# Eight PSUM banks shared out anew in a two-layer transformer kernel with three attentions

## The chip, the cores and the metric

The kernel runs on one core of one Trainium2 chip. The metric is the device time of one execution in microseconds; for the kernel before, three executions are known.

## The reference

64 sequences of 128 tokens with 128 features pass through two layers. The first has three parts: self-attention with rotary embedding, cross-attention to 77 context tokens, and an MLP; the second is one more cross-attention. Each part starts with a layer norm, scaled and shifted per sequence. Cut to what matters:

```python
def attn(q, k, v, mask):                      # 16 heads of 8 features
    s = einsum('bqhd,bkhd->bhqk', q, k) / sqrt(8)
    s = where(mask, s, lowest)
    return einsum('bhqk,bkhd->bqhd', softmax(s), v)

x = x + g_msa * (attn(rope(xn @ Wq), rope(xn @ Wk), xn @ Wv, mask) @ Wo)   # 128 keys
x = x + g_x   * (attn(xc @ cq, ctx @ ck, ctx @ cv, kv_mask) @ co)          # 77 keys
x = x + g_mlp * (gelu(xm @ W1 + b1) @ W2 + b2)
x = x + attn(xq @ Wq1 + bq, cn @ Wk1 + bk, cn @ Wv1 + bv) @ Wp + bp        # 77 keys
```

## The kernel before

The activations stay in SBUF, features on partitions (`c.xt`). `two_layers` calls phases one after the other; each is a block with one program per engine, written out by hand in order and joined by semaphores. There are setup, load, norms, three attentions (named `sa`, `ca` and `xa`; the text calls them the first, second and third), the MLP and the store.

An attention works in **groups** of 4 sequences (16 groups), **steps** of one sequence (4 per group) and **units** of half a step, 8 of the 16 heads (8 per group, 128 in all). The loops on all engines run over the same number `u`, here called slot; slot `8i + n` is the n-th slot of group i. In slot u the engines do this:

- TensorE: for even u `turn_max` (line 446) transposes the row maxima of a step; `natural(u + 3)` (line 419) makes scores with the queries on partitions, for the maxima alone; `transposed(u)` (line 452) makes the scores again with the keys on partitions and adds the negated maxima; `values(u - 1)` (line 477) multiplies the exponentials of the unit before with the values; and `project` (line 394) does one projection, where the table `slot_jobs` (line 375) has one.
- ScalarE: for even u `keep_max` (line 605), `exponentials(u)` (line 618), for even u `invert` (line 611, two instructions for 1/sum), in slot 8i `take_values` (line 593, four copies of the projected values into `vz`), and parts of splitting q and k into bf16 pieces.
- VectorE: `maxima(u + 3)` (line 530), `read_out` of a step in odd slots (line 539, `den` and `vv` out of the values' bank), and `take` or `add_out` (lines 509, 547), which read a projection of slot u - 1.
- GpSimd splits the maxima and q and k into pieces and multiplies `vv` with 1/sum (`normalise`, line 661). SyncE moves the pieces of q and k into `stacks`, group by group.

The projections of a group stand in these slots: in the first attention `q`, `qr`, `k`, `kr` (`r` for the rotated ones) in slots 0 to 3 for the group two further on, in the other two `q` in slot 1 and `k` in slot 3; in all of them `o`, the output projection of the group before, in slot 5, and `v`, the values of the next group, in slot 7.

The 8 PSUM banks: a pair `ps_nat` for the first scores, a pair `ps_st` for the transposed ones, two banks `ps_pj` that projections take in turn, and two `ps_po` that steps take in turn for the values' output, with the transposed maxima in the same bank. Who waits for whom on TensorE follows from that:

```python
if number[job] >= 2:                      # project: the reader of the job two before
    before, ib = jobs[number[job] - 2]
...
if u > 0:                                 # transposed: the exponentials of the unit before
    pe.wait_ge(exped, u)
...
if step >= 2:                             # values: step - 2 read out
    pe.wait_ge(po_read, step - 1)
```

Of the kernel before, what the change touches and what calls it, by code (L numbers as in the profile page):

```python
# [29 lines left out]
H, HD = 16, 8  # L30
# [316 lines left out]
def attention_phase(nc, c, name, ctx, *, nk, kv_src, wq, wk, wv, wo, rotate=False, q_bias=None,  # L347
# [38 lines left out]
    takes = {job: n for n, job in enumerate(j for j in jobs if j[0] in kinds)}  # L386
    pj = lambda job: c.ps_pj[number[job] % 2]

    with nc.Block() as block:
        @block.tensor  # L390
        def _(pe):
            t = nc.tensor

            def project(job):
                kind, i = job
                if number[job] >= 2:
                    before, ib = jobs[number[job] - 2]
# [48 lines left out]
            def turn_max(step):  # L446
                pe.wait_ge(max_split, 4 * step + 4)
                if step >= 2:
                    pe.wait_ge(po_read, step - 1)
                t.transpose(c.turned_max[step % 2], c.nm[:, step % 2, :], c.eye_bf[:]).then_inc(max_turned, 1)  # L450

            def transposed(u):
                step, p = u // 2, u % 2
                i, j = step // G, step % G
                par = i % NB
                if u > 0:
                    pe.wait_ge(exped, u)
                if pair_mask:
                    for h in range(2):
                        t.matmul(c.ps_st[h][0:nk, :], c.eye_bf[:], c.mask_t[:].unsqueeze(1).broadcast_to([128, 4, S]),  # L460
                                 start=True, stop=False, skip_group_check=True)
                for g in range(4):
                    for h in range(2):
                        at = pair(2 * p, g)
                        t.matmul(c.ps_st[h][0:nk, S * g:S * g + S], kst[half(h), par, at, nk * j:nk * j + nk],  # L465
                                 qst[half(h), par, at, S * j:S * j + S],
                                 start=g == 0 and not pair_mask, stop=False, skip_group_check=True)
                if p == 0:
                    pe.wait_ge(max_kept, step + 1)
                for g in range(4):  # L470
                    for h in range(2):
                        m = t.matmul(c.ps_st[h][0:nk, S * g:S * g + S], c.pick_bf[half(h), 4 * (2 * p + h) + g:4 * (2 * p + h) + g + 1].broadcast_to([64, nk]),  # L472
                                     c.mt[half(h), step % 2, :], start=False, stop=g == 3, skip_group_check=True)
                        if g == 3:
                            m.then_inc(st_full, 1)

            def values(u):
# [28 lines left out]
        def _(dve):  # L506
            v = nc.vector

            def take(job):
                kind, i = job  # L510
                x = 0 if kind[0] == "q" else 1
                bank = pj(job)
                dve.wait_ge(pj_full, number[job] + 1)
# [25 lines left out]
            def read_out(step):  # L539
                bank = c.ps_po[step % 2]  # L540
                dve.wait_ge(pv_done, 2 * step + 2)
# [5 lines left out]
            def add_out(i):  # L547
                job = ("o", i)
                dve.wait_ge(pj_full, number[job] + 1)
                if gate is None:  # L550
                    xs = c.xt[:, NT * i:NT * i + NT]
                    v.scalar_tensor_tensor(out=xs, in0=pj(job)[:], scalar=out_bias, in1=xs, op0=ALU.add, op1=ALU.add).then_inc(added, 1)
                else:
                    for b in range(G):
                        n = G * i + b
                        xs = c.xt[:, S * n:S * n + S]
                        v.scalar_tensor_tensor(out=xs, in0=pj(job)[:, S * b:S * b + S], scalar=c.mod[:, gate, n:n + 1],
                                               in1=xs, op0=ALU.mult, op1=ALU.add).then_inc(added, 1)
# [18 lines left out]
        def _(act):  # L577
# [15 lines left out]
            def take_values(i):  # L593
                job = ("v", i)
                act.wait_ge(pj_full, number[job] + 1)
                if i >= 2:
                    act.wait_ge(pv_done, PER * (i - 1))
                src = pj(job)[0:nk, :].rearrange("p (b t f) -> p b t f", b=G, t=H // 2)
                for hh in range(4):
# [5 lines left out]
            def keep_max(step):  # L605
                act.wait_ge(max_turned, step + 1)
                if step >= 2:
                    act.wait_ge(st_full, 4 * (step - 1))
                a.activation(c.mt[:, step % 2, :], c.turned_max[step % 2], ACT.Copy).then_inc(max_kept, 1)  # L609

# [7 lines left out]
            def exponentials(u):  # L618
# [4 lines left out]
                bias = c.key_bias[0:nk, step:step + 1] if key_mask else 0.0  # L623
                a.activation(c.p[0:nk, 2 * p:2 * p + 2, :].rearrange("p h n -> p (h n)"), c.st_pair[0:nk, :], ACT.Exp, bias=bias).then_inc(exped, 1)  # L624

# [199 lines left out]
def two_layers(nc, ins, out):  # L825
    with ExitStack() as ctx:
# [68 lines left out]
        c.ps_nat = [c.nat_pair[:, 0:512], c.nat_pair[:, 512:1024]]  # L895
        c.ps_st = [c.st_pair[:, 0:512], c.st_pair[:, 512:1024]]
        c.ps_pj = [ps("ps_pj0"), ps("ps_pj1")]

        c.ps_po = [ps("ps_po0"), ps("ps_po1")]
        c.turned_max = [bank[:, 2 * S:2 * S + S // 2].bitcast(BF16) for bank in c.ps_po]  # L900
        c.turned_mask = c.ps_po[0][:].bitcast(BF16)

# [60 lines left out]
```

## Time and profile before

| | us |
|---|---|
| median of 3 runs | 1566.06 |
| lowest and highest run | 1566.05, 1567.51 |
| the profiled execution | 1563.82 |
| its span | 1562.2 |
| TensorE busy (matmuls) | 1337.8 |
| ScalarE busy | 905.3 |
| VectorE busy | 805.7 |
| GpSimd busy | 688.2 |

The profiled execution is one execution of its own; its time is 2.2 us below the median and 1.6 above its span. Busy time counts overlapping instructions once. PE is TensorE, PEld its weight loads, ACT ScalarE, DVE VectorE, POOL GpSimd. "Idle before" is the time in which an engine did nothing ahead of an instruction, with what ended it. An instruction's recorded end can overlap the next one's start by a few hundredths of a us.

### The profile page before, as it was taken

Reading aid. Unit: us, or ns where it says so; the run is one execution under the profiler, and the core shown is the slowest. Engines: PE = TensorE matmul, PEld = TensorE weight load, DVE = VectorE, ACT = ScalarE, POOL = GpSimd, SP = SyncE. Lnnn points to the kernel's source line nnn. Section 1 sums busy time; section 2 is a strip of 40 time slices with the busy share of each in tenths; the row PEclk is TensorE's granted clock in tenths of the full one; section 3 lists DMA queues with packets and bytes.
Section 4 is the critical chain, followed back from the end, with each engine's and each line's share of the span. In section 5 each row is a group of like instructions: output and inputs, shape, how many; then the busy total and the mean of one; then the engine's idle time right before and its main releaser. Section 6 shows DMA issues by size and latency. Waiting matters only on the chain. (4 is left out here: it accounts for less than half of the span.)

```text
span 1562.2 us, 44242 instructions
## 1 busy us (share of the span) xinstructions
PE 1337.8 (86%) x17952; PEld 746.4 (48%) x17952; DVE 805.7 (52%) x1772; ACT 905.3 (58%) x1692; POOL 688.2 (44%) x1405
## 2 busy tenths in 40 slices
PE   2584999999999988499999998889987488888885
PEld 2531555555555442255555555334433355555563
DVE  4263565656665546255555554522167355565553
ACT  0171555555555547277777777644476477777773
POOL 0004556565656520466666663001100566666640
PEclk9996999999999999699999999899998799999996
DMA  2502534344343500444444442000000555555423
GB/s 82 151 1 54 101 64 92 73 84 82 73 92 63 102 2 1 87 89 84 83 84 83 81 83 37 0 0 0 0 1 1 99 93 100 95 96 92 89 46 108
DMA packets 136124, 103.44 MB, mean 66 GB/s; under 512 B 13913, under 2 KB 135666, under 8 KB 135922
## 3 DMA queue, kind: packets, MB, share of 16 engines
q1 hardware_dynamic: 135922, 100.62, 32.8%
q8 instruction: 142, 2.33, 0.6%
q14 instruction: 60, 0.49, 0.1%
HBM read 9.08 MB, written 4.19 MB: 8 GB/s over the span
## 5 line engine op out<-in xcount | busy, mean ns | idle before, releaser
L535 DVE TENSOR_REDUCE negmax<-ps_nat 128x8 f32<-128x616 f32 (+1 forms) x384 | 361.1, 940 | 403.8 <-PE ps_nat L442 159.9
L624 ACT ACTIVATE p<-ps_st 128x1024 f32<-128x1024 f32 (+1 forms) x256 | 260.5, 1018 | 181.5 <-PE ps_st L472 179.5
L489 PE MATMUL ps_po<-p,vz 77*32 77x128 f32 (+1 forms) x6144 | 248.5, 279 | 26.6 <-issue 24.6
L431 PE MATMUL ps_nat<-stacks 64*128 64x77 bf16 (+1 forms) x3072 | 134.2, 209 | 58.0 <-DMA stacks<-parts 51.7
L667 POOL TENSOR_TENSOR ot<-vv,den 128x256 f32<-128x256 f32 x192 | 139.5, 727 | 100.4 <-ACT den L616 99.3
L465 PE MATMUL ps_st<-stacks 64*77 64x128 bf16 (+1 forms) x3072 | 158.0, 223 | 24.7 <-ACT p L624 22.4
L489 PEld LDWEIGHTS ps_po<-p,vz 77*32 77x32 f32 (+1 forms) x6144 | 145.9, 109 | 64.2 <-issue 29.9
L624 ACT ACTIVATE p<-ps_st,key_bias 77x1024 f32<-77x1024 f32 x128 | 141.5, 1105 | 59.9 <-PE ps_st L472 59.7
L653 POOL CAST nm<-negmax 128x32 bf16<-128x32 f32 x192 | 40.0, 209 | 289.9 <-DVE negmax L535 289.8
L431 PEld LDWEIGHTS ps_nat<-stacks 64*128 64x128 bf16 x3072 | 78.1, 97 | 179.3 <-issue 147.0
L679 POOL TENSOR_TENSOR whole<-whole,parts 128x512 f32<-128x512 f32 x96 | 98.3, 1024 | 137.4 <-ACT parts L587 137.4
L465 PEld LDWEIGHTS ps_st<-stacks 64*77 64x77 bf16 (+1 forms) x3072 | 97.1, 107 | 127.5 <-issue 68.7
L472 PE MATMUL ps_st<-mt,pick_bf 64*77 64x128 bf16 (+1 forms) x3072 | 151.7, 219 | 0.0
L609 ACT ACTIVATE mt<-ps_po 128x128 bf16<-128x128 bf16 x192 | 52.8, 275 | 128.3 <-PE ps_po L450 128.2
L472 PEld LDWEIGHTS ps_st<-mt,pick_bf 64*77 64x77 bf16 (+1 forms) x3072 | 106.9, 108 | 2.5 <-ACT mt L609 0.3
L408 PE MATMUL ps_pj<-ot,wo 128*128 128x512 f32 x192 | 100.4, 648 | 7.1 <-POOL ot L667 7.1
L687 POOL TENSOR_TENSOR parts<-whole,parts 128x512 bf16<-128x512 f32 x96 | 98.5, 1026 | 0.0
L674 POOL TENSOR_TENSOR whole<-part 128x512 f32<-128x512 f32 x32 | 40.6, 1269 | 121.7 <-DVE part L519 121.7
L680 POOL COPY parts<-parts 128x1024 bf16<-128x1024 bf16 x96 | 88.4, 921 | 0.0
L544 DVE STREAM_SHUFFLE den<-ps_po 128x256 f32<-128x256 f32 x192 | 85.7, 446 | 0.0
L616 ACT ACTIVATE den<-den 128x256 f32<-128x256 f32 x192 | 80.0, 417 | 6.1
L587 ACT ACTIVATE parts<-whole 128x512 bf16<-128x512 f32 x96 | 53.6, 559 | 50.0 <-DMA stacks<-parts 29.5
(142 smaller groups left out, 2144.0 us busy)
## 6 DMA issues: line engine op xcount, KB each, us to landing
stacks<-parts SPq DMA_DIRECT2D x512, 128.0 KB, 3.2
stacks<-parts SPq DMA_DIRECT2D x256, 77.0 KB, 2.6
p<-in_x_dram SPq DMA_DIRECT2D x16, 256.0 KB
out_dram<-p SPq DMA_DIRECT2D x16, 256.0 KB, 2.4
p<-in_ctx_dram SPq DMA_DIRECT2D x16, 154.0 KB
ht<-in_L_xcond_adaLN_W_dram SPq DMA_DIRECT2D x1, 576.0 KB
w<-in_L_xcond_mlp_W_dram SPq DMA_DIRECT2D x2, 256.0 KB
wqkv<-in_L_xcond_qkv_W_dram SPq DMA_DIRECT2D x1, 192.0 KB
```

Of the source, the lines that this page charges most:

```text
L408: m = t.matmul(bank[:], wo[:, p, :], c.ot[:, i % 2, p, :], start=p == 0, stop=p == 1)
L431: m = t.matmul(c.ps_nat[h][:, nk * g:nk * g + nk], qst[half(h), par, at, S * j:S * j + S], kst[half(h), par, at, nk * j:nk * j + nk], star ...
L465: t.matmul(c.ps_st[h][0:nk, S * g:S * g + S], kst[half(h), par, at, nk * j:nk * j + nk], qst[half(h), par, at, S * j:S * j + S], start=g = ...
L472: m = t.matmul(c.ps_st[h][0:nk, S * g:S * g + S], c.pick_bf[half(h), 4 * (2 * p + h) + g:4 * (2 * p + h) + g + 1].broadcast_to([64, nk]), ...
L489: m = t.matmul(bank[32 * g:32 * g + 32, S * p:S * p + S], c.vz[0:nk, i % 2, j, g, 32 * hh:32 * hh + 32], c.p[0:nk, hh, S * g:S * g + S], s ...
L535: v.tensor_reduce(c.negmax[:, step % 2, 8 * p:8 * p + 8].rearrange("p (h g) -> p h g", h=2), c.nat_pair[:].rearrange("p (h n) -> p h n", h ...
L544: v.stream_shuffle(c.den[:, step % 2, :], bank[:, 0:2 * S], DEN_ROWS).then_inc(den_here, 1)
L624: a.activation(c.p[0:nk, 2 * p:2 * p + 2, :].rearrange("p h n -> p (h n)"), c.st_pair[0:nk, :], ACT.Exp, bias=bias).then_inc(exped, 1)
L667: p.tensor_tensor(c.ot[:, i % 2, :, S * j:S * j + S], c.vv[:, step % 2, :].rearrange("q (p n) -> q p n", p=2), c.den[:, step % 2, :].rearr ...
L679: p.tensor_tensor(c.whole[:, x, w], c.whole[:, x, w], c.parts[:, x, hi[0], w], ALU.subtract).then_inc(rest, 1)
L680: p.tensor_copy(c.parts[:, x, hi[1]:hi[2] + 1:hi[2] - hi[1], w], c.parts[:, x, hi[0]:hi[0] + 1, w].broadcast_to([128, 2, width[x]]))
L687: p.tensor_tensor(c.parts[:, x, LOW[x], w], c.whole[:, x, w], c.parts[:, x, md[0], w], ALU.subtract).then_inc(split[x], 1)
```

## The change

The transposed scores get two pairs of banks that units take in turn (`c.st[u % 2]`), the values' output one bank (`c.po`, the transposed maxima with it) and the projections one bank (`c.pj`). The waits follow: `transposed(u)` waits for the exponentials of unit u - 2 instead of u - 1; `values` for the read-out of step - 1 instead of step - 2; `project` for the reader of the last job instead of the last but one. VectorE's `read_out` moves to the front of its slot, ahead of `take` (first attention) and `maxima`. The phases outside the attentions use the same banks under other names. The core of the diff:

```diff
-    pj = lambda job: c.ps_pj[number[job] % 2]
...
             def project(job):
                 kind, i = job
-                if number[job] >= 2:
-                    before, ib = jobs[number[job] - 2]
+                if number[job] >= 1:
+                    before, ib = jobs[number[job] - 1]
                     if before == "v":
                         pe.wait_ge(values_kept, ib + 1)
                     elif before == "o":
                         pe.wait_ge(added, N_ADD * (ib + 1))
                     else:
                         pe.wait_ge(taken, takes[before, ib] + 1)
-                bank = pj(job)
+                bank = c.pj
...
-                t.transpose(c.turned_max[step % 2], c.nm[:, step % 2, :], c.eye_bf[:]).then_inc(max_turned, 1)
+                t.transpose(c.turned_max, c.nm[:, step % 2, :], c.eye_bf[:]).then_inc(max_turned, 1)
...
             def transposed(u):
-                if u > 0:
-                    pe.wait_ge(exped, u)
+                if u > 1:
+                    pe.wait_ge(exped, u - 1)
...
-                        t.matmul(c.ps_st[h][0:nk, S * g:S * g + S], kst[half(h), par, at, nk * j:nk * j + nk],
+                        t.matmul(c.st[u % 2][h][0:nk, S * g:S * g + S], kst[half(h), par, at, nk * j:nk * j + nk],
...
             def values(u):
-                    if step >= 2:
-                        pe.wait_ge(po_read, step - 1)
-                bank = c.ps_po[step % 2]
+                    if step >= 1:
+                        pe.wait_ge(po_read, step)
+                bank = c.po
...
             for u in range(FIRST, LAST):
+                if in_range(u - 2) and u % 2 == 1 and u >= 3:
+                    read_out((u - 3) // 2)
                 if rotate and u - 1 in slot_jobs:
                     read(slot_jobs[u - 1])
                 if in_range(u + AHEAD):
                     maxima(u + AHEAD)
-                if in_range(u - 2) and u % 2 == 1 and u >= 3:
-                    read_out((u - 3) // 2)
                 if not rotate and u - 1 in slot_jobs:
                     read(slot_jobs[u - 1])
...
-        c.nat_pair = ctx.enter_context(nc.psum_tensor("ps_nat", [128, 1024], F32))
-        c.st_pair = ctx.enter_context(nc.psum_tensor("ps_st", [128, 1024], F32))
-        c.ps_pj = [ps("ps_pj0"), ps("ps_pj1")]
-        c.ps_po = [ps("ps_po0"), ps("ps_po1")]
+        pairs = [ctx.enter_context(nc.psum_tensor("ps_" + n, [128, 1024], F32)) for n in ("nat", "st0", "st1", "rest")]
+        halves = lambda pair: [pair[:, 0:512], pair[:, 512:1024]]
+        c.ps_nat, c.ps_st, c.ps_pj = halves(pairs[0]), halves(pairs[1]), halves(pairs[2])
+        c.st = [halves(pairs[1]), halves(pairs[2])]
+        c.po, c.pj = halves(pairs[3])
```

How this moves instructions and waits is best seen in two places. The first is TensorE's queue in the first attention, slot 8 (scores, values of unit 7, projection of `q`, then the next `natural`), with the semaphores that each waits for. Before:

```order
L460 MATMUL ps_st<-mask_t,eye_bf 128x512 [waits sa_exped]
...
L472 MATMUL ps_st<-mt,pick_bf 128x128 [waits sa_max_kept]
...
L489 MATMUL ps_po1<-p,vz 32x128 [waits sa_exped]
...
L416 MATMUL ps_pj0<-ht,wqkv 128x512 [waits sa_taken]
L431 MATMUL ps_nat<-stacks 128x128 [waits sa_maxed]
...
L489 MATMUL ps_po0<-p,vz 32x128 [waits sa_po_read,sa_values_kept,sa_exped]
...
L416 MATMUL ps_pj1<-ht,wrot 128x512 [waits sa_values_kept]
```

And changed (every line number is one lower, `ps_rest` holds `po` and `pj`):

```order
L459 MATMUL ps_st0<-mask_t,eye_bf 128x512 [waits sa_exped]
...
L471 MATMUL ps_st0<-mt,pick_bf 128x128 [waits sa_max_kept]
...
L488 MATMUL ps_rest<-p,vz 32x128 [waits sa_exped]
...
L415 MATMUL ps_rest<-ht,wqkv 128x512 [waits sa_values_kept]
L430 MATMUL ps_nat<-stacks 128x128 [waits sa_maxed]
...
L488 MATMUL ps_rest<-p,vz 32x128 [waits sa_po_read,sa_values_kept,sa_exped]
...
L415 MATMUL ps_rest<-ht,wrot 128x512 [waits sa_taken]
```

No matmul has moved; the wait for `values_kept` (ScalarE's `vz`) has moved from `qr` to `q`, ahead of the next `natural`.

The second place is VectorE's queue in the third attention, slots 8i+1 to 8i+3. Before:

```order
L535 TENSOR_REDUCE negmax<-ps_nat 128x8 [waits xa_max_split,xa_nat_full]
L544 STREAM_SHUFFLE den<-ps_po1 128x256 [waits xa_out_ready,xa_pv_done]
L545 COPY vv<-ps_po1 128x256
L535 TENSOR_REDUCE negmax<-ps_nat 128x8 [waits xa_nat_full]
L526 TENSOR_SCALAR whole<-ps_pj0,vec 128x512 [waits xa_split_q,xa_pj_full]
L535 TENSOR_REDUCE negmax<-ps_nat 128x8 [waits xa_max_split,xa_nat_full]
L544 STREAM_SHUFFLE den<-ps_po0 128x256 [waits xa_out_ready,xa_pv_done]
L545 COPY vv<-ps_po0 128x256
```

And changed:

```order
L543 STREAM_SHUFFLE den<-ps_rest 128x256 [waits xa_out_ready,xa_pv_done]
L544 COPY vv<-ps_rest 128x256
L534 TENSOR_REDUCE negmax<-ps_nat 128x8 [waits xa_max_split,xa_nat_full]
L534 TENSOR_REDUCE negmax<-ps_nat 128x8 [waits xa_nat_full]
L525 TENSOR_SCALAR whole<-ps_rest,vec 128x512 [waits xa_split_q,xa_pj_full]
L543 STREAM_SHUFFLE den<-ps_rest 128x256 [waits xa_out_ready,xa_pv_done]
L544 COPY vv<-ps_rest 128x256
L534 TENSOR_REDUCE negmax<-ps_nat 128x8 [waits xa_max_split,xa_nat_full]
```

The read-out (shuffle and copy) has passed the reduction of its slot; the reading of a projection, here `q`, stands ahead of it as before.

## Rows read from the trace of the kernel before

**Rows 1.** The page's busy times: engine, busy us (share of the span), instructions.
```profile
PE 1337.8 (86%) x17952; PEld 746.4 (48%) x17952; DVE 805.7 (52%) x1772; ACT 905.3 (58%) x1692; POOL 688.2 (44%) x1405
```

**Rows 2.** Waits in total (us, times, longest), then the group of line 450 (busy | idle).
```profile
PEld ps_st L465 <- ACT p L624: 57.6, 139, 1.0
...
L450 PE MATMUL ps_po<-eye_bf,nm 128*128 128x128 bf16 x192 | 42.5, 221 | 3.8 <-DVE vv L545 3.7
```

**Rows 3.** TensorE's timeline, first attention: projections of `q`. Columns: start, us.
```profile
158.81 1.13 PE L416 MATMUL ps_pj<-ht,wqkv 128*128 128x512 f32 x2
...
265.04 1.13 PE L416 MATMUL ps_pj<-ht,wqkv 128*128 128x512 f32 x2
...
506.81 1.12 PE L416 MATMUL ps_pj<-ht,wqkv 128*128 128x512 f32 x2
```

**Rows 4.** ScalarE's timeline, first attention, in the same slots.
```profile
159.87 0.78 ACT L601 ACTIVATE vz<-ps_pj 128x128 f32<-128x128 f32 x4
...
264.60 1.02 ACT L624 ACTIVATE p<-ps_st 128x1024 f32<-128x1024 f32 x1 [1.60 <-PE ps_st L472]
...
266.28 0.76 ACT L601 ACTIVATE vz<-ps_pj 128x128 f32<-128x128 f32 x4
...
508.05 0.76 ACT L601 ACTIVATE vz<-ps_pj 128x128 f32<-128x128 f32 x4
```

**Rows 5.** Timeline, first attention: a read-out that TensorE waits for.
```profile
175.32 0.41 DVE L545 COPY vv<-ps_po 128x256 f32<-128x256 f32 x1
...
175.88 0.22 PE L450 MATMUL ps_po<-eye_bf,nm 128*128 128x128 bf16 x1 [0.53 <-DVE vv L545]
```

**Rows 6.** TensorE's timeline, third attention, slots 8i+2, 8i+3, 8i+5, 8i+7.
```profile
1421.66 0.32 PE L431 MATMUL ps_nat<-stacks 64*128 64x77 bf16 x8
...
1422.44 0.65 PE L489 MATMUL ps_po<-p,vz 77*32 77x128 f32 x16
1423.02 0.32 PE L431 MATMUL ps_nat<-stacks 64*128 64x77 bf16 x8
1423.65 0.42 PE L465 MATMUL ps_st<-stacks 64*77 64x128 bf16 x8 [0.32 <-ACT p L624]
...
1424.22 0.64 PE L489 MATMUL ps_po<-p,vz 77*32 77x128 f32 x16
...
1428.19 0.64 PE L489 MATMUL ps_po<-p,vz 77*32 77x128 f32 x16
...
1433.29 0.65 PE L489 MATMUL ps_po<-p,vz 77*32 77x128 f32 x16
```

**Rows 7.** VectorE's timeline, third attention, the same stretch.
```profile
1422.77 0.74 DVE L526 TENSOR_SCALAR whole<-ps_pj,vec 128x512 f32<-128x512 f32 x1
...
1424.14 0.45 DVE L544 STREAM_SHUFFLE den<-ps_po 128x256 f32<-128x256 f32 x1
1424.49 0.40 DVE L545 COPY vv<-ps_po 128x256 f32<-128x256 f32 x1
...
1426.68 0.53 DVE L528 TENSOR_SCALAR whole<-ps_pj,vec 128x308 f32<-128x308 f32 x1
...
1431.83 0.74 DVE L552 SCALAR_TENSOR_TENSOR xt<-ps_pj,bp,xt 128x512 f32<-128x512 f32 x1
```

**Rows 8.** Timeline, second attention: VectorE's `add_out` and TensorE's values, slot 8i+7.
```profile
751.94 1.12 DVE L557 SCALAR_TENSOR_TENSOR xt<-ps_pj,mod,xt 128x128 f32<-128x128 f32 x4
...
753.56 0.64 PE L489 MATMUL ps_po<-p,vz 77*32 77x128 f32 x16
```

**Rows 9.** TensorE's gap in the timeline, then windows: us, busy times, PEclk (1.00 is 2.4 GHz).
```profile
547.35 0.61 PE L431 MATMUL ps_nat<-stacks 64*128 64x128 bf16 x8 [2.42 <-DMA stacks<-parts]
...
547.20:550.60 3.40, 3.25 (x28) 1.58 (x28) 1.64 (x4) 0.00 (x0) 0.00 (x0) 0.50 0.02 5
584.75:588.10 3.35, 3.35 (x4) 0.90 (x4) 0.00 (x0) 0.00 (x0) 0.00 (x0) 0.50 0.00 0
1475.65:1479.00 3.35, 3.35 (x35) 1.59 (x27) 0.43 (x1) 0.67 (x2) 0.00 (x0) 0.50 0.72 132
```

More of the change, by code:

```diff
@@ L455, in transposed @@
                 par = i % NB
[L456 to L457 removed]
+                if u > 1:
+                    pe.wait_ge(exped, u - 1)
                 if pair_mask:
                     for h in range(2):
[L460 removed]
+                        t.matmul(c.st[u % 2][h][0:nk, :], c.eye_bf[:], c.mask_t[:].unsqueeze(1).broadcast_to([128, 4, S]),
                                  start=True, stop=False, skip_group_check=True)
@@ L471, in transposed @@
                     for h in range(2):
-                        m = t.matmul(c.ps_st[h][0:nk, S * g:S * g + S], c.pick_bf[half(h), 4 * (2 * p + h) + g:4 * (2 * p + h) + g + 1].broadcast_to([64, nk]),
+                        m = t.matmul(c.st[u % 2][h][0:nk, S * g:S * g + S], c.pick_bf[half(h), 4 * (2 * p + h) + g:4 * (2 * p + h) + g + 1].broadcast_to([64, nk]),
                                      c.mt[half(h), step % 2, :], start=False, stop=g == 3, skip_group_check=True)
@@ L511, in take @@
                 x = 0 if kind[0] == "q" else 1
-                bank = pj(job)
+                bank = c.pj
                 dve.wait_ge(pj_full, number[job] + 1)
@@ L539, in read_out @@
             def read_out(step):
-                bank = c.ps_po[step % 2]
+                bank = c.po
                 dve.wait_ge(pv_done, 2 * step + 2)
@@ L551, in add_out @@
                     xs = c.xt[:, NT * i:NT * i + NT]
-                    v.scalar_tensor_tensor(out=xs, in0=pj(job)[:], scalar=out_bias, in1=xs, op0=ALU.add, op1=ALU.add).then_inc(added, 1)
+                    v.scalar_tensor_tensor(out=xs, in0=c.pj[:], scalar=out_bias, in1=xs, op0=ALU.add, op1=ALU.add).then_inc(added, 1)
                 else:
@@ L556, in add_out @@
                         xs = c.xt[:, S * n:S * n + S]
-                        v.scalar_tensor_tensor(out=xs, in0=pj(job)[:, S * b:S * b + S], scalar=c.mod[:, gate, n:n + 1],
+                        v.scalar_tensor_tensor(out=xs, in0=c.pj[:, S * b:S * b + S], scalar=c.mod[:, gate, n:n + 1],
                                                in1=xs, op0=ALU.mult, op1=ALU.add).then_inc(added, 1)
@@ L608, in keep_max @@
                     act.wait_ge(st_full, 4 * (step - 1))
-                a.activation(c.mt[:, step % 2, :], c.turned_max[step % 2], ACT.Copy).then_inc(max_kept, 1)
+                a.activation(c.mt[:, step % 2, :], c.turned_max, ACT.Copy).then_inc(max_kept, 1)
             def invert(step):
@@ L623, in exponentials @@
                 bias = c.key_bias[0:nk, step:step + 1] if key_mask else 0.0
-                a.activation(c.p[0:nk, 2 * p:2 * p + 2, :].rearrange("p h n -> p (h n)"), c.st_pair[0:nk, :], ACT.Exp, bias=bias).then_inc(exped, 1)
+                a.activation(c.p[0:nk, 2 * p:2 * p + 2, :].rearrange("p h n -> p (h n)"), c.st_pairs[u % 2][0:nk, :], ACT.Exp, bias=bias).then_inc(exped, 1)
             steps = (((4, 0, split_high), (6, 0, split_mid), (6, 1, split_high), (8, 1, split_mid)) if rotate
@@ L892, in two_layers @@
         c.vec_row = VEC_ROW
-        c.nat_pair = ctx.enter_context(nc.psum_tensor("ps_nat", [128, 1024], F32))
-        c.st_pair = ctx.enter_context(nc.psum_tensor("ps_st", [128, 1024], F32))
-        c.ps_nat = [c.nat_pair[:, 0:512], c.nat_pair[:, 512:1024]]
-        c.ps_st = [c.st_pair[:, 0:512], c.st_pair[:, 512:1024]]
-        c.ps_pj = [ps("ps_pj0"), ps("ps_pj1")]
-        c.ps_po = [ps("ps_po0"), ps("ps_po1")]
-        c.turned_max = [bank[:, 2 * S:2 * S + S // 2].bitcast(BF16) for bank in c.ps_po]
-        c.turned_mask = c.ps_po[0][:].bitcast(BF16)
+        pairs = [ctx.enter_context(nc.psum_tensor("ps_" + n, [128, 1024], F32)) for n in ("nat", "st0", "st1", "rest")]
+        halves = lambda pair: [pair[:, 0:512], pair[:, 512:1024]]
+        c.vec_row = VEC_ROW
+        c.nat_pair, c.st_pairs = pairs[0], pairs[1:3]
+        c.ps_nat, c.ps_st, c.ps_pj = halves(pairs[0]), halves(pairs[1]), halves(pairs[2])
+        c.st = [halves(pairs[1]), halves(pairs[2])]
+        c.po, c.pj = halves(pairs[3])
+        c.turned_max = c.po[:, 2 * S:2 * S + S // 2].bitcast(BF16)
+        c.turned_mask = c.po.bitcast(BF16)
         setup_phase(nc, c, ins, ctx)
```

2 lines of the change are left out of this document (1 added, 1 removed).

## The prediction

> **What bounds the kernel now.** I read the page's busy shares first: TensorE is busy for 86% of the span [rows 1], more than any other engine, so only time that TensorE spends waiting can be won, and every wait added to its queue is paid. Then I read the waits and the grouped instructions, since the change is meant to loosen one wait of TensorE, the one for the exponentials (`exped`). The wait that can be seen is small: 57.6 us of idle weight loads in 139 waits, and where the matmuls themselves idle the timeline of the third attention puts it at 0.32 us each [rows 2, 6]. The first attention has none of it in its steady groups: its timeline of TensorE is closed, and the project of `q` in slot 8i follows the values without a gap [rows 3]. So the gain can only lie in the second and third attention, and anything that holds TensorE in the first one goes to the end of the kernel in full.
>
> **The bank of the projections, first attention.** Before, a projection waits for the reader of the projection two before it. Now it waits for the last one. The projections stand in slots 0, 1, 2, 3 (`q`, `qr`, `k`, `kr`), 5 (`o`) and 7 (`v`) of each group, and only one neighbour matters: `v` of slot 8i-1 is read by ScalarE in slot 8i (`take_values`, line 601), and there it stands behind the exponential of the same slot and the two instructions of `invert`. `q` of slot 8i must now wait for it, where only `qr`, a slot later, did. In the group shown ScalarE starts its exponential at 264.60 and the four copies to `vz` at 266.28, which end 0.76 later at 267.04 [rows 4]. `q` started at 265.04 [rows 3]. The handover from a reader to the next matmul took 0.15 us where VectorE's copy ended at 175.73 and TensorE started at 175.88 [rows 5]. The new stall is 267.04 + 0.15 - 265.04 = 2.15 us. It comes for `v` 0 to 13, 14 times; the first one is 159.87 + 0.78 + 0.15 - 158.81 = 1.99, the last (508.05 against 506.81) is 2.15 again [rows 3, 4]. Together 1.99 + 13 x 2.15 = **29.9 us**. ScalarE can't come earlier, since its chain starts when TensorE has filled the scores of slot 8i, which stands ahead of `q`. Queued behind `q` are the maxima's scores for VectorE and the scores of slot 8i+1, so nobody works in the gap. Bounds: 14 x 2.00 = 28 without any handover, 14 x 2.35 = 33 with 0.2 more for a weight load that can't be hidden.
>
> The other pairs have room. `qr` waits for `take` of `q`, which VectorE does (0.7 us) while TensorE does a whole slot of some 3.5 us; `v` waits for `add_out` of slot 6. In the second and third attention `q` stands in slot 8i+1, behind the values of step 4i, which wait for the same `vz` already: nothing is added there.
>
> **What the gap does to TensorE's clock.** The granted clock is at 2.4 GHz through nearly all of the first attention. After its one long gap, 2.42 us for the stacks, it fell to 1.2 GHz for 3.4 us, and in the third attention it fell once after a gap of 0.81 us [rows 9], while about 30 gaps of that size stand in the second and third attention. The other gap of its kind, at the end of this attention, was followed by 1.2 GHz too, the window from 584.75 on [rows 9]. My gaps of 2.15 us are nearer to the 2.42 that brought the clock down than to the 0.81 that mostly didn't. I take 9 falls in 14. A fall costs at most half of 3.4 us, 1.7; I take 1.6, because work bound by weight loads slows less. Together 9 x 1.6 = **14.4 us**; bounds 0 and 14 x 1.7 = 24. The Trainium skill (TensorE: Matmul & The Clock Gate, section HAM oscillation) holds only idle stretches longer than any of these for dangerous; by it this term is nothing, and the sum would be 14.4 lower. The trace does not agree with it for the gap of 2.42.
>
> **The second pair of banks for the scores, third attention.** In a slot with an even number TensorE goes from the first scores to the values in 1422.44 - 1421.66 = 0.78 us; in an odd one, where it waits for the exponential, it takes 1424.22 - 1423.02 = 1.20 [rows 6]. So 0.42 us could be won in odd slots. But the values of the odd slot now have another wait, `po_read`: there is one bank for their output, and VectorE must have read out the step before. VectorE's two read-out instructions take 1424.49 + 0.40 - 1424.14 = 0.75 us, and in its queue they stand behind what it does in the slot before. The next instruction on VectorE starts some 0.07 us ahead of the recorded end of the one before. Slot 3: behind `take` of `q`, which ends at 1422.77 + 0.74 - 0.07 = 1423.44; read out by 1424.19, values at 1424.34 instead of 1424.22: 0.12 lost. Slot 5: behind `take` of `k`, 1426.68 + 0.53 - 0.07 = 1427.14, so 1428.04 instead of 1428.19: 0.15 won. Slot 7: behind `add_out`, 1431.83 + 0.74 - 0.07 = 1432.50, so 1433.40 instead of 1433.29: 0.11 lost [rows 6, 7]. Slot 1: the values wait for `vz`, on the same ScalarE chain as before: nothing. That is 0.08 lost per group, 15 groups, **1.2 us**. Bound on the good side: 3 x 0.42 x 15 = 19 us won, if VectorE were in time everywhere. That the read-out stands ahead of the maxima costs VectorE's reduction up to 0.75 us, but TensorE needs it only after the projection of that odd slot, so it stays hidden.
>
> The Trainium skill (Perfetto Trace Analysis, section Matmuls) wants independent groups of matmuls rotated through different banks, so that reading one overlaps filling the next. The change follows this for the scores and gives it up for the values and the projections; by this case's rows the second weighs more.
>
> **Second attention.** The same walk for slot 7: `add_out` is four instructions of 1.12 us together, ends at 751.94 + 1.12 - 0.07 = 752.99, and the values come at 752.99 + 0.75 + 0.15 = 753.89 instead of 753.56 [rows 8]: 0.33 lost. Slots 3 and 5 have room and win their wait for the exponential, which is too short to show as idle of the matmuls; I take 0.1 each. 0.13 x 15 = **2.0 us** lost.
>
> **Ends of the phases.** The transposed maxima waited 3.8 us in all for VectorE's `vv`, in groups that lack a projection [rows 2]; with the read-out first in its slot these waits go, but about a third of them stand ahead of a wait for the stacks that takes them back: 2.5 won. The first steps of the third attention win about 1 more. At the start of the first attention `qr` must wait for `take` of `q`, one reading of 0.7 us and a handover: 1 us lost. Net **2.5 us won**. Norms, MLP and store only change names of banks: nothing.
>
> **The sum.** 29.9 + 14.4 + 1.2 + 2.0 - 2.5 = 45.0 us. On the profiled execution's 1563.82 that is 1608.8. The median of the runs is 2.2 above that execution, so the forecast is 1566.06 + 45.0 = **1611 us**, 2.9% slower.
>
> **The rivals.**
> First, the clock holds in the gaps (3 falls or fewer). For it: some 30 gaps of 0.81 us with one or two falls. Against: the one gap of over 2 us inside this attention. Time: 1611 - 14 = 1597. Its condition is also the skill's rule named above. Chance 0.23.
> Second, the clock falls after every gap: 1611 + 8 to 10 = 1620. For it: both long gaps of this attention were followed by 1.2 GHz. Chance 0.14.
> Third, on the other side: the scores run ahead and every wait for the exponential is won back, at all four odd slots of a group in both later attentions, 15 x 4 x (0.42 + 0.1) = 31, and with the 3.7 at the ends 35, while the clock holds: 1566 + 30 - 35 = 1561, a little faster. For it: these waits are in the trace and the second pair takes them away. Against: VectorE's queue in slots 3 and 7 [rows 7, 8] and `vz` in slot 1. It decides only from a winning of over 0.5 us per odd slot, which is more than these rows hold. Chance 0.05.
> That the second pair does nothing because the values of slot u-1, right behind the scores of slot u, wait for the same exponential is contained in the forecast: it holds for the first attention, where no such wait was.
>
> **How the numbers follow.** The forecast's own case, 4 to 12 falls, has 0.5 and spans 1602 to 1617. The rest, 0.08, is for terms off in size, a third of it within no change. The range takes the first rival with some slack for the bound of 19 us in the third attention, and most of the second: 1590 to 1622. A change under 0.2%, 3 us, can't be told from none in a measurement of this kernel. Faster by more: 0.05 (the third rival). Within: 0.03. Slower by more: 0.92.
>
> **What would show it.** Right: in the first attention TensorE idles some 2 us ahead of `q` of slot 8i, 14 times, released by ScalarE's `vz`; a group there is 29.0 us long instead of 26.9 ((506.81 - 265.04) / 9 from [rows 3]), or some 30.6 where the clock falls behind the gap; rows of 1.2 GHz right behind several of these gaps; in the third attention no idle ahead of the scores for the exponential, but 0.3 to 0.5 ahead of the values, released by VectorE's copy of `vv`; and a group there as long as before within 0.2 us. Wrong: if `q` does not idle, if groups of the third attention are shorter by over 0.5 us, or if the clock stays at 2.4 GHz through the whole first attention.

## The result, and the profile after

| | before | changed |
|---|---|---|
| median, us | 1566.78 | 1610.13 |
| lowest to highest, runs | 1566.05 to 1568.03, 4 | 1606.38 to 1617.32, 4 |
| the profiled execution | 1563.82 | 1609.02 |

The changed kernel is slower: the ratio is 1.0285 with a 95% interval of 1.026 to 1.0309. The forecast was 1611, and 1608.8 for the profiled execution.

To see where the time went I cut both timelines of TensorE into the three attentions, each from its first projection to the start of its last output projection:

| us | before | changed | difference |
|---|---|---|---|
| first attention | 463.88 | 509.52 | +45.6 |
| second attention | 352.10 | 352.09 | 0.0 |
| third attention | 323.35 | 323.13 | -0.2 |

All of the loss lies in the first attention. The waits of the changed kernel, in total (us, times, longest), name most of it:

```profile
PEld ps_rest L415 <- ACT vz L600: 31.4, 14, 2.3
...
PEld ps_rest L488 <- ACT p L623: 30.7, 50, 1.1
...
PE ps_rest L415 <- ACT vz L600: 27.7, 14, 2.0
...
PE ps_rest L488 <- DVE vv L544: 25.9, 61, 0.5
...
PE ps_rest L488 <- ACT vz L600: 21.5, 17, 1.3
```

Line 415 is the projection, line 488 the values. The third row is the new stall, 14 times and 2.0 us at most. The fourth is the other new wait, for VectorE's read-out. The wait of the scores' weight loads for the exponentials, 57.6 us before [rows 2], has all but gone (3.9 us are left); 30.7 us of a wait for the same instruction now stand ahead of the values. The transposed maxima, line 450 before with 3.8 us of idle time [rows 2], have none left:

```profile
L449 PE MATMUL ps_rest<-eye_bf,nm 128*128 128x128 bf16 x192 | 42.7, 222 | 0.0
```

TensorE's timeline of the first attention (start, duration, in brackets the idle time before), the first four projections of `q` in the slots of [rows 3]:

```profile
164.47 1.12 PE L415 MATMUL ps_rest<-ht,wqkv 128*128 128x512 f32 x2 [1.82 <-ACT vz L600]
...
193.08 1.12 PE L415 MATMUL ps_rest<-ht,wqkv 128*128 128x512 f32 x2 [1.99 <-ACT vz L600]
...
222.00 1.12 PE L415 MATMUL ps_rest<-ht,wqkv 128*128 128x512 f32 x2 [1.99 <-ACT vz L600]
...
252.49 1.12 PE L415 MATMUL ps_rest<-ht,wqkv 128*128 128x512 f32 x2 [1.99 <-ACT vz L600]
```

and ScalarE's copies to `vz` ahead of two of them:

```profile
192.27 0.76 ACT L600 ACTIVATE vz<-ps_rest 128x128 f32<-128x128 f32 x4
...
221.19 0.76 ACT L600 ACTIVATE vz<-ps_rest 128x128 f32<-128x128 f32 x4
```

The copies end at 193.03 and 221.95, and `q` starts 0.05 us later. From 193.08 to 222.00 a group takes 28.92 us, from 222.00 to 252.49 it takes 30.49. Before, a group took 26.86. The difference between the two lengths of now is 1.57, and the view of windows says what it is. Its columns: stretch, length; busy time (instructions) of PE, PEld, DVE, ACT, POOL; granted clock; DMA share; GB/s.

```profile
194.10:197.50 3.40, 3.40 (x47) 1.76 (x47) 1.92 (x2) 1.02 (x1) 1.23 (x2) 1.00 0.78 149
223.60:226.90 3.30, 3.30 (x36) 1.67 (x34) 1.48 (x2) 0.70 (x1) 0.66 (x1) 0.50 0.76 143
252.70:256.10 3.40, 3.40 (x47) 1.57 (x47) 1.92 (x2) 0.82 (x2) 1.73 (x2) 1.00 0.78 165
```

Behind the gaps that end at 193.08 and 252.49 the clock stays at 2.4 GHz, behind the one that ends at 222.00 it is at 1.2, and a stretch of about the same length holds 36 matmuls in place of 47. Such a stretch of some 3.4 us follows 11 of the 14 gaps.

The third attention, where [rows 6, 7] were read, on TensorE:

```profile
1418.68 1.98 PE L407 MATMUL ps_rest<-ot,wo 128*128 128x512 f32 x4
...
1428.41 0.64 PE L488 MATMUL ps_rest<-p,vz 77*32 77x128 f32 x16 [1.32 <-ACT vz L600]
...
1432.76 0.65 PE L488 MATMUL ps_rest<-p,vz 77*32 77x128 f32 x16 [0.54 <-DVE vv L544]
...
1436.56 0.65 PE L488 MATMUL ps_rest<-p,vz 77*32 77x128 f32 x16 [0.33 <-DVE vv L544]
1437.14 1.98 PE L407 MATMUL ps_rest<-ot,wo 128*128 128x512 f32 x4
...
1441.77 0.64 PE L488 MATMUL ps_rest<-p,vz 77*32 77x128 f32 x16 [0.54 <-DVE vv L544]
```

and VectorE ahead of the values at 1432.76:

```profile
1431.20 0.74 DVE L525 TENSOR_SCALAR whole<-ps_rest,vec 128x512 f32<-128x512 f32 x1
...
1431.87 0.44 DVE L543 STREAM_SHUFFLE den<-ps_rest 128x256 f32<-128x256 f32 x1
1432.21 0.41 DVE L544 COPY vv<-ps_rest 128x256 f32<-128x256 f32 x1
```

These are `take` of `q`, shuffle and copy. The copy ends at 1432.62, and the values start 0.14 us later. The idle 1.32 us at 1428.41 is the wait for `vz` in slot 8i+1; before, TensorE idled there for 0.81 us. The scores no longer wait, the values do. A group takes 1437.14 - 1418.68 = 18.46 us against 18.41 before (output projections at 1391.93 and 1410.34 there).

### The profile page after: what moved, and what is told of

It is laid out like the page before. It is cut to its first block and busy times, and to the rows that moved or that the text cites. A ratio compares the mean times of both kernels' runs of the same rounds, so it can differ in the third digit from the quotient of the medians.

```text
span 1607.4 us, 44245 instructions
## 1 busy us (share of the span) xinstructions
PE 1354.0 (84%) x17952; PEld 750.4 (47%) x17952; DVE 807.1 (50%) x1772; ACT 904.6 (56%) x1692; POOL 687.8 (43%) x1405
## 5 line engine op out<-in xcount | busy, mean ns | idle before, releaser
L488 PE MATMUL ps_rest<-p,vz 77*32 77x128 f32 (+1 forms) x6144 | 249.2, 280 | 63.5 <-DVE vv L544 25.9
L488 PEld LDWEIGHTS ps_rest<-p,vz 77*32 77x32 f32 (+1 forms) x6144 | 148.2, 109 | 104.1 <-issue 47.1
L608 ACT ACTIVATE mt<-ps_rest 128x128 bf16<-128x128 bf16 x192 | 52.9, 276 | 131.5 <-PE ps_rest L449 131.4
L407 PE MATMUL ps_rest<-ot,wo 128*128 128x512 f32 x192 | 98.7, 638 | 7.1 <-POOL ot L666 7.1
L298 PE MATMUL ps_st<-xt,centre 128*128 128x512 f32 x128 | 72.1, 658 | 16.9 <-DVE p L338 10.0
L543 DVE STREAM_SHUFFLE den<-ps_rest 128x256 f32<-128x256 f32 x192 | 84.8, 441 | 0.0
L438 PE MATMUL ps_nat<-mask_nat,eye_bf 128*128 128x512 bf16 x256 | 84.0, 412 | 0.0
```

Of the source, the lines that this page charges most:

```text
L488: m = t.matmul(bank[32 * g:32 * g + 32, S * p:S * p + S], c.vz[0:nk, i % 2, j, g, 32 * hh:32 * hh + 32], c.p[0:nk, hh, S * g:S * g + S], s ...
L543: v.stream_shuffle(c.den[:, step % 2, :], bank[:, 0:2 * S], DEN_ROWS).then_inc(den_here, 1)
```

## The experiments

Every kernel was timed beside the kernel before on the same chip. Three series were run; the median of before was 1567.41 in the first, 1564.31 in the second and 1565.29 in the third, so where kernels of different series are compared, the difference of the ratios stands beside that of the medians. A kernel "as the changed one, but" has its line numbers from there.

### One projection bank alone

The kernel before with one edit: both names of projection banks lead to one bank, and the wait follows.

```diff
-    pj = lambda job: c.ps_pj[number[job] % 2]
+    pj = lambda job: c.ps_pj[0]
...
-                if number[job] >= 2:
-                    before, ib = jobs[number[job] - 2]
+                if number[job] >= 1:
+                    before, ib = jobs[number[job] - 1]
```

> Only the projections' bank changes: one bank in place of two, each projection waits for the reader of the last one; scores, values' output and VectorE's order stay as before. My theory (the loss is q waiting for vz in the first attention, and the clock falling behind that gap): nearly the whole loss is here. First attention about 45 us longer, 14 gaps of 2.0 us ahead of q, some 11 of them followed by 1.2 GHz; second and third as before; 1605 to 1618 us in all. Rival (the loss comes from the values' single bank or from the new order on VectorE): within 3 us of before, 1567.

Measured: 1616.53 (1614.27 to 1618.55), ratio 1.0336 [1.0305, 1.0366]: 49 us above before by the medians, 53 by the ratio. The waits:

```profile
PEld ps_st L465 <- ACT p L624: 57.9, 139, 1.0
...
PE ps_pj L416 <- ACT vz L601: 27.7, 14, 2.0
```

The first row is nearly as before (57.6), the second is the changed kernel's stall to the tenth of a microsecond; 12 gaps are followed by 1.2 GHz. The first attention takes 513.54 us, 49.7 more than before. The third was 4.3 us longer in this execution as well: nearly all of its groups are as long as before, 18.42 us, but more stretches of 1.2 GHz stand among them. So one bank for the projections explains the loss by itself. What the rest of the change does looks like a small net gain, but the intervals of the two ratios just overlap.

### One values bank alone

The kernel before with one bank for the values' output and the read-out first in its slot; the two projection banks and the one pair for the scores stay.

```diff
-                    if step >= 2:
-                        pe.wait_ge(po_read, step - 1)
+                    if step >= 1:
+                        pe.wait_ge(po_read, step)
...
+                if in_range(u - 2) and u % 2 == 1 and u >= 3:
+                    read_out((u - 3) // 2)
                 if rotate and u - 1 in slot_jobs:
...
-                if in_range(u - 2) and u % 2 == 1 and u >= 3:
-                    read_out((u - 3) // 2)
...
-        c.ps_po = [ps("ps_po0"), ps("ps_po1")]
+        c.ps_po = [ps("ps_po0")] * 2
```

> Only the values' output changes: one bank in place of two, with VectorE's read-out first in its slot; the projections keep two banks, the scores one pair. My theory: nothing in the first attention; in the second 0.33 us more in slot 7 (5 us), in the third 0.1 more in slots 3 and 7 (3.5 us), 2.5 us won where the transposed maxima waited for vv: 1570 to 1575. Rival (the read-out always has room): 1564. Rival (the single bank costs in the first attention too): 1580 or more.

Measured: 1570.92 (1569.24 to 1576.31, 10 runs), ratio 1.0035 [1.0017, 1.0053]. The first attention is 2.1 us shorter than before, the second 3.9 longer, the third 4.5 longer. A group of the second attention takes 20.69 us in place of 20.36, 0.33 more. The timeline of the second attention shows the wait in slot 7, where `add_out` stands ahead of the read-out, beside the wait for the exponentials, which is still there (second fence, the waits):

```profile
753.80 0.65 PE L489 MATMUL ps_po<-p,vz 77*32 77x128 f32 x16 [0.25 <-DVE vv L545]
```

```profile
PE ps_st L465 <- ACT p L624: 24.1, 68, 0.9
```

By the ratios one bank costs 5 us for the values and 53 us for the projections (3.5 and 49 by the medians).

### The second pair of score banks taken back

The changed kernel with one pair for the transposed scores, and its wait.

```diff
-                if u > 1:
-                    pe.wait_ge(exped, u - 1)
+                if u > 0:
+                    pe.wait_ge(exped, u)
...
-        c.nat_pair, c.st_pairs = pairs[0], pairs[1:3]
+        c.nat_pair, c.st_pairs = pairs[0], [pairs[1], pairs[1]]
...
-        c.st = [halves(pairs[1]), halves(pairs[2])]
+        c.st = [halves(pairs[1]), halves(pairs[1])]
```

> The changed kernel with its second pair of banks for the transposed scores taken back (they wait for the exponentials of the unit before again). My theory: the second pair is worth little, since the values wait for VectorE's read-out or for vz nearly as long: 0.1 to 0.15 us in slots 3 and 5 of the later attentions, 3 to 6 us in all, so 1612 to 1617 with the spread that the clock gives. Rival (the second pair wins its 0.42 us per odd slot and hides a larger loss of the single banks): 20 us or more above the changed kernel, 1630 or more.

Measured: 1622.18 (1621.6 to 1623.88), ratio 1.0374 [1.0346, 1.0402]: 12 us above the changed kernel by the medians, 14 by the ratios. The first attention is as long as in the changed kernel (509.84 against 509.52), the second 3.6 us longer, the third 8.8. The waits for ScalarE are back, and those for VectorE have nearly gone behind them:

```profile
PE ps_rest L488 <- DVE vv L544: 3.5, 14, 0.3
...
PE ps_st L464 <- ACT p L623: 22.3, 62, 0.9
```

So the second pair does what it says, and is worth 12 us or more here, two to four times what I had expected. Much of the 8.8 is the clock. At the start of the third attention it stays at 1.2 GHz longer, so that the first `k` inside the slots comes 36.43 us behind the first projection instead of 33.90. Behind that, up to the gap ahead of the last output projection, it falls to 1.2 GHz 6 times where in the changed kernel it falls 3 times, and a group of this attention with such a stretch takes 1.2 us more (19.68 against 18.46). That makes 2.5 + 3 x 1.2 = 6.1; the waits by themselves would then be worth 3.6 + 2.7 = 6.3. This is read from one execution of each kernel and not tested by itself.

### The gap filled

Does the gap cost only its own length, or the clock too? The changed kernel with nine more matmuls of 512 columns ahead of the projection of `q`, which write to a bank that the next scores overwrite. They are extra work that the reference doesn't have; none of the kernel's own is left out.

```diff
                     values(u - 1)
+                if rotate and u % PER == 0 and 0 <= u <= PER * (NG - 3):
+                    for _ in range(9):
+                        t.matmul(c.st[(u + 1) % 2][0], c.eye_bf[:], c.mask_t[:].unsqueeze(1).broadcast_to([128, 4, S]),
+                                 start=True, stop=True, skip_group_check=True)
```

> The changed kernel with nine more matmuls of 512 columns ahead of q in the 14 slots in which it waits for vz; they write into the pair of banks for the next transposed scores, which start anew there, so the result stays. They take some 1.9 us, as long as the gap. My theory: the wait stays as long, but the clock no longer falls, so the first attention is 16 to 18 us shorter than in the changed kernel and the time is 1590 to 1597 (0 to 2 rows of 1.2 GHz in the steady groups). Rival (the time above the gaps comes from something else that follows the stall): 1605 to 1615, as the changed kernel.

Measured: 1595.69 (1594.22 to 1599.93), ratio 1.0209 [1.0172, 1.0245]: 14.4 us below the changed kernel by the medians, 12 by the ratios. The timeline:

```profile
216.21 2.12 PE L503 MATMUL ps_st<-mask_t,eye_bf 128*128 128x512 bf16 x9
218.26 1.13 PE L415 MATMUL ps_rest<-ht,wqkv 128*128 128x512 f32 x2
...
245.13 2.12 PE L503 MATMUL ps_st<-mask_t,eye_bf 128*128 128x512 bf16 x9
247.19 1.12 PE L415 MATMUL ps_rest<-ht,wqkv 128*128 128x512 f32 x2
```

The useless matmuls fill the gap, `q` comes when it did, and the group is 247.19 - 218.26 = 28.93 long, as long as with an empty gap (28.92). But no steady group has 1.2 GHz in it any more, and the first attention is 18.4 us shorter. The clock's term is thereby measured apart from the stall. The time as a whole gains less than 18.4, since the third attention was 3.7 us longer in this execution, most of it by more time at 1.2 GHz.

### The reader brought forward

If what costs is `vz` behind an exponential, then `take_values` in front of it should cure the first attention, with one bank for the projections. I made the edit in both kernels:

```diff
                         keep_max(u // 2)
+                    if at == 0 and i - 2 in range(NG):
+                        take_values(i - 2)
                     exponentials(u)
...
                     invert((u - 4) // 2)
-                if at == 0 and i - 2 in range(NG):
-                    take_values(i - 2)
```

The changed kernel with it:

> The changed kernel with ScalarE's four copies to vz moved ahead of the exponential of their slot (behind the copy of the transposed maxima). My theory: vz is there about 0.7 us after v, before q wants its bank; the first attention loses its 14 gaps and its falls of the clock (45 us), and in the later attentions the values of slot 8i+1 no longer wait for vz (0.8 us and part of the wait for the exponential, 31 groups: 25 to 35 us). 1532 to 1543 us. Rival (q has another reason to wait, or the exponential comes later by the 0.7 us of the copies and TensorE waits for it in turn): 1565 or more.

The kernel before with it:

> The kernel before with the same move of the copies to vz, nothing else. My theory: nothing in the first attention, 0.8 us in each group of the later ones, 25 us: 1541 to 1545 us. If the second pair of banks is of use once vz is early, the changed kernel with the move is faster than this one by 3 to 8 us; if the single banks for values and projections cost more than it wins, it is slower by up to 5. Rival (the copies delay the exponential and nothing is won): 1565.

Measured: the changed kernel 1537.32 (1536.56 to 1544.83), ratio 0.9827 [0.9791, 0.9862]; the kernel before 1539.24 (1538.36 to 1541.22), ratio 0.9827 [0.9794, 0.9859]. Both are faster than either kernel without the edit, the second one by slightly more than I had expected. ScalarE of the changed one, then its TensorE:

```profile
263.35 0.28 ACT L608 ACTIVATE mt<-ps_rest 128x128 bf16<-128x128 bf16 x1 [0.39 <-PE ps_rest L449]
263.52 0.78 ACT L600 ACTIVATE vz<-ps_rest 128x128 f32<-128x128 f32 x4
265.23 1.02 ACT L623 ACTIVATE p<-ps_st 128x1024 f32<-128x1024 f32 x1 [0.93 <-PE ps_st L471]
```

```profile
265.67 1.12 PE L415 MATMUL ps_rest<-ht,wqkv 128*128 128x512 f32 x2
...
292.53 1.13 PE L415 MATMUL ps_rest<-ht,wqkv 128*128 128x512 f32 x2
```

The copies to `vz` end at 264.30, 1.37 us ahead of `q`, in time in which ScalarE waits for scores anyway (0.93 us are left). The gap is gone and the group is 26.86 long again. The gain of the changed kernel over before lies in the later attentions: the second takes 337.09 and the third 313.31 us, 15.0 and 10.0 less. There the values of slot 8i+1 had waited 1.32 us for `vz` (the row at 1428.41 above), and all 3 falls of the clock among the groups of the third attention had come behind that wait; now the wait is gone, no fall is left between 1248 and 1472 us, and the longest wait is another:

```profile
1350.74 0.32 PE L430 MATMUL ps_nat<-stacks 64*128 64x77 bf16 x8 [0.97 <-DMA stacks<-parts]
...
1352.02 1.98 PE L407 MATMUL ps_rest<-ot,wo 128*128 128x512 f32 x4
...
1356.65 0.65 PE L488 MATMUL ps_rest<-p,vz 77*32 77x128 f32 x16 [0.54 <-DVE vv L544]
...
1368.41 0.32 PE L430 MATMUL ps_nat<-stacks 64*128 64x77 bf16 x8 [0.57 <-DMA stacks<-parts]
...
1369.68 1.98 PE L407 MATMUL ps_rest<-ot,wo 128*128 128x512 f32 x4
```

This group takes 17.66 us; the others between 1263 and 1458 us take 17.4 to 18.2. In the kernel before the edit wins 12.0 us in the second attention, 8.5 in the third, and 2.7 in the first, where I had expected nothing.

Is the new sharing of banks of any use once the reader is early? Both kernels again, in the third series.

The changed one:

> The changed kernel with the copies to vz early once more, beside the kernel before with the same move, in five rounds. If the second pair of banks is of use, this one is 2 to 4 us faster; rival: no difference beyond 1 us.

The one of before:

> The kernel before with the copies to vz early once more: 1538 to 1541 us; see the run beside it.

Measured: 1539.49 (1535.3 to 1543.97), ratio 0.983 [0.9805, 0.9855], and 1541.63 (1537.3 to 1543.14), ratio 0.9839 [0.9814, 0.9863]. The difference between the two kernels is 2 us in the same direction both times, but the intervals overlap, so it isn't shown. By the profiles the new sharing wins 3.0 to 3.6 us in the second attention and 1.5 in the third, and loses 1.6 to 2.0 in the first, whose start runs slower (below).

### Two attempts to win the read-out's wait

What is left of the change's cost in the later attentions is the wait for the read-out behind `take` of `q` and `k`. With `q` and `k` in slots 0 and 2, their readers stand elsewhere in VectorE's queue. The early-reader version of the changed kernel, with:

```diff
-    at_slot = dict(zip(kinds, range(4) if rotate else (1, 3)))
+    at_slot = dict(zip(kinds, range(4) if rotate else (0, 2)))
```

> The changed kernel with vz early, and in the second and third attention q and k projected in slots 0 and 2 in place of 1 and 3, so that VectorE reads them in odd slots behind the read-out, not in even slots ahead of it. My theory: the waits of the values for vv in slots 3 and 5 of the third attention go (0.54 and 0.33 us of idle each), but the wait for the stacks in slot 5 (1.1 us now) takes it back, since the splitting of q and k stays where it was: within 3 us of the same kernel without this step, 1534 to 1541. Rival (the read-out's wait is what bounds the third attention): 1520 to 1527.

Measured: 1542.46 (1542.02 to 1543.84), ratio 0.9854 [0.9833, 0.9875]: no gain over 1539.49. The waits for the read-out fell from 28.0 us in 68 to 17.1 in 43, but other waits took their place. The longest is an idle time of 1.24 to 1.35 us ahead of the first scores, for which the trace names no releaser, and three times in the third attention the clock fell behind it. So the read-out's wait alone was not what bound that attention.

Then the splits of ScalarE and GpSimd one slot earlier as well, so that the stacks come sooner:

```diff
-                     else ((2, 0, split_high), (4, 0, split_mid), (4, 1, split_high), (6, 1, split_mid)))
+                     else ((1, 0, split_high), (3, 0, split_mid), (3, 1, split_high), (5, 1, split_mid)))
...
-                     else ((3, 0, take_high), (5, 0, take_mid), (5, 1, take_high), (7, 1, take_mid)))
+                     else ((2, 0, take_high), (4, 0, take_mid), (4, 1, take_high), (6, 1, take_mid)))
```

> As the run before it, with ScalarE's and GpSimd's splitting of q and k one slot earlier as well in the second and third attention, so that the stacks come earlier. My theory (once vz is early, the stacks and the read-out bound the third attention together): both waits go, some 1 us per group and the odd slots of ScalarE are less empty: 1518 to 1530. Rival (ScalarE's splits in odd slots push its exponential, or the stacks are not bound by the splits): 1534 or more.

Measured: 1563.78 (1561.11 to 1571.73, 10 runs), ratio 0.9991 [0.9975, 1.0008]. A clear miss of the 1518 to 1530 that I had expected, and 21 us slower than the version without it. The rows of ScalarE, then of TensorE:

```profile
1422.15 0.63 ACT L586 ACTIVATE parts<-whole 128x512 bf16<-128x512 f32 x1
1422.68 0.26 ACT L608 ACTIVATE mt<-ps_rest 128x128 bf16<-128x128 bf16 x1
```

```profile
1423.00 0.42 PE L471 MATMUL ps_st<-mt,pick_bf 64*77 64x128 bf16 x8 [0.75 <-ACT mt L608]
```

A split of an odd slot now stands ahead of `keep_max` (line 608) of the next even slot, and TensorE waits for the maxima, 58 times and 36.0 us in all; that wait had been 5.2 us in the version without it and 1.5 in the changed kernel. It is the case's own mistake over again, on the same engine: work put in front of a reader that TensorE needs.

## Why the prediction was right

**The stall of `q`**: right in place, releaser and number. Forecast 2.15 us each; the longer groups give 28.92 - 26.86 = 2.06, which is 0.07 more than the idle time shown. With 1.82 + 0.07 = 1.89 for the first that is 13 x 2.06 + 1.89 = 28.7 us against 29.9. What was too large is the handover: 0.15 us by the row of VectorE's copy, 0.05 behind ScalarE's. That ScalarE can't come earlier was wrong as it was put. Its exponential can't, but the copies to `vz` need not stand behind it: put in front they ended 1.37 us ahead of `q`.

**The clock**: right in kind, undersized. 11 gaps brought the clock down where I had taken 9, at 1.57 us each where I had taken 1.6: 17.3 against 14.4. The filled gap gives 18.4 for the same thing. The first rival, that the clock holds, is refuted in this attention: a gap of 2.0 us was followed by 1.2 GHz in 11 of 14 cases, and filling it removed that. The rule of the Trainium skill (TensorE: Matmul & The Clock Gate, section HAM oscillation) warns only of longer idle stretches; by it this term would have been nothing, and the trace does not agree. In the third attention of the kernel before, where I had counted one fall behind a gap of 0.81 us, there were two, at 1475.65 and at 1496.1. The second rival, a fall after every gap, was closer than its chance of 0.14 says.

**The start of the first attention**: undersized. I had one projection wait for one reading, 1 us. All seven behind the first waited 0.78 us each for `take`, and the whole start ran at 1.2 GHz, where the one of before had come up to 2.4 by its third projection, 3.2 us behind the start of the first:

```profile
124.28 2.08 PE L415 MATMUL ps_rest<-ht,wrot 128*128 128x512 f32 x2 [0.79 <-DVE part L518]
127.14 2.07 PE L415 MATMUL ps_rest<-ht,wqkv 128*128 128x512 f32 x2 [0.78 <-DVE part L518]
```

The first scores came 150.51 - 121.45 = 29.06 us behind the first projection, against 26.19 before: 2.9 us lost. The one bank is what does it: with one projection bank alone it takes 29.09 us and the start runs at 1.2 GHz in the same way, with one values bank alone it takes 26.48 and the clock comes up. Which part of it is the waits' own length, and that the clock stayed down because of them, is argued from the order of events; no run took that apart.

**The ends**: forecast 3.5 us won over the three attentions; in the first alone it was 2.5. From the last of the 14 `q` to the output projection at the end it took 76.85 us against 77.80, with a fall of the clock of 1.57 in it. Together 28.7 + 17.3 + 2.9 - 2.5 = 46.4; 45.6 were measured. Of the 0.8 between them most lies in the first group: from `q` to `q` it took 28.61 us (193.08 - 164.47), and 25.64 before, 2.97 more where a stall and a fall make 3.63.

**The later attentions**: forecast 2.0 and 1.2 us lost, measured 0.0 and -0.2. The mechanism is as told: idle time moved from the scores to the values, 0.54 and 0.33 us, released by `vv`. The terms of a group were right or nearly so: a group of the second attention takes 20.47 us against 20.36, 0.11 more where I had 0.13, and one of the third 18.46 against 18.41, 0.05 more where I had 0.08. The experiments show both halves of the first: one values bank alone makes 20.69, the 0.33 forecast for slot 7, and the second pair gives back 0.22 where I had 0.2. What I had not counted are the ends of the second attention. Its last groups have fewer projections, and two of them take 18.91 and 18.76 us where they took 19.26 each; with the start some 1.3 us are won there, as much as the groups lose. In the third attention the first output projection comes 55.65 us behind the first projection in place of 56.84, the 1 us that I had put under the ends. In all, one values bank without the second pair loses 8.4 us in the two attentions, with one more fall of the clock in it than before; with the second pair nothing is lost.

The stall and the later attentions were forecast too large by 4.6 us together, the clock and the start too small by 4.8. That they cancel is luck, and so is part of the closeness of 1611 to 1610.13.

**The third rival**, a winning of 0.5 us in every odd slot, fell where the profile had spoken against it: the wait for the exponentials went, and the wait for the read-out stood in its place. The changed kernel does come out faster than the one of before once `vz` is early, but so does the kernel before (1539.24), so that gain is not the banks'.

## What to carry to other kernels

When banks are shared out anew, ask of each consumer that is left with one bank where its reader stands in its engine's queue: here one bank cost 5 us where the reader could be put first in its slot, and 53 us where it stood behind an exponential. Moving a reader in front of long work that waits anyway cost nothing that shows here, and in the kernel before it was worth 24 to 25 us, more than any sharing of the banks here. And count a gap in a closed timeline of TensorE with what the clock does behind it: a stall of 2.06 us cost 2.06 + 1.57 in most groups.

## What the hardware showed that I had not expected

That gaps of 2.0 us bring the clock to 1.2 GHz was in the forecast, how regularly was not: 11 of 14 in the changed kernel, 12 of 14 with one projection bank alone. The gaps, and the work ahead of them, are the same; what differs is when they come. In the record of the granted clock one fall comes 0.17 us behind the start of the `q` at 281.41, and in each following group 0.2 to 0.3 us later, up to 1.65 us behind the one at 464.25; the next `q`, at 494.69, has none. With one projection bank alone there is such a row too, from 0.06 us at 372.44 to 1.59 at 555.23. Why is left open.

The changed kernel's runs go from 1606.38 to 1617.32, 0.7%. The mean granted clock of the four runs goes with their time: 0.939 in the run of 1606.38, 0.935 at 1609.02, 0.933 at 1611.24 and 0.929 at 1617.32. A stretch of 3.4 us at half the clock takes 3.4 x 0.5 / 1607 = 0.0011 from the mean, so 0.010 is some 9 falls, which at 1.2 to 1.57 us each make 11 to 14; the runs differ by 10.9. So the number of falls would account for the spread; where they lay is known for the profiled run alone. It is not a mark of the changed kernel only: the four runs of the kernel before beside it spread by 0.1%, but its 13 runs in the first series go from 1559.53 to 1570.76, with the clock at 0.954 and 0.949.

Among the groups of the third attention the clock falls now and then behind a shorter gap: 3 times behind the 1.32 us that the changed kernel waits for `vz`, twice behind the 0.81 us of the kernel before, 6 times behind the same 0.81 us with the second pair taken back. The changed kernel and the one with the gap filled have the same instructions there, and took 323.13 and 326.79 us. Between kernels that differ by 2 us, that is enough to hide which is better.
